# Seven-product value projections in the second half of block 1 as well, with sums of the context made in block 0

## The chip, the cores and the metric

The kernel runs on one core of one Trainium2 chip. The metric is the device time of one execution in microseconds, the median of three runs. Engines are named as in the profile: PE is TensorE (its weight loads are PEld), DVE is VectorE, ACT is ScalarE, POOL is GpSimd, and SP is SyncE, which issues nearly all transfers (its rows are marked SPq).

## The reference

```python
# x: 32 x 64 x 512, ctx: 32 x 64 x 512, H = 32 heads of DH = 128
q = (layernorm(x) @ Wq).reshape(b, lq, h, dh)
k = (ctx @ Wk).reshape(b, lk, h, dh)
v = (ctx @ Wv).reshape(b, lk, h, dh)
score = einsum('bqhd,bkhd->bhqk', q, k) * scale + position_bias   # masked keys: -inf
probs = softmax(score)                                            # masked keys: 0
x = x + tanh(g_xattn) * (einsum('bhqk,bkhd->bqhd', probs, v).reshape(b, lq, h * dh) @ Wo)
x = x + tanh(g_ffn) * (layernorm(x) @ weight.T + bias + lora(layernorm(x)))
```

The part that the change touches is `v`: the context (512 columns) times `Wv` (512 x 4096).

## The kernel before

**Precision.** Each float32 operand of a product is split into a high part (rounded by ACT, `hi`) and a rest (subtracted by DVE or POOL, `lo`, L1426 on POOL and L1151 on DVE). A product takes three matmuls: high times high, high times rest, rest times high (`mm3`, L395 to L398).

**Blocks and slots.** The 2048 rows are four blocks of 512 (8 batches). For each block the 32 heads are gone through, one head to a slot: 128 slots, slot n is head n % 32 of block n // 32. In a slot PE does the queries (12 matmuls of 128x512), the keys (12), then "main jobs" (24 matmuls: either two tiles of values for a group of four heads, or two tiles of the output projection), some small jobs in some slots (turning the normalised rows for the next block or the feed-forward part, the LoRA part, the dense part), then the scores of head n and last the attention of head n - 1. In block 0 the weights come raw from HBM, are split, used, and written back to HBM in split form (`wq_split` and so on); the later blocks load the split forms. So in slots 0 to 31 ACT and POOL also split each head's query and key weights, and in two slots of four POOL splits two chunks of the next group's value weights (`weights_v`).

**Programs by hand.** Each engine has its own instruction stream, written slot by slot, and waits on semaphores. In ACT's slot n come, in this order: the high part of the values of head n - 1 (`head_values`, v_hi), of the queries, of the next query weights, of the value or output weights, of the keys, of the next key weights, then the probabilities of head n - 1 (pt), a piece of the context or of the feed-forward weights, the first part of a round (below), copies of values out of PSUM, the turned rows, half the attention result (attn), the exponentials of head n, and the high part of the attention (ot_hi). In POOL's slot: the bias plus mask (L1466), the rest of the values (v_lo, L1485), the rests of the weights, of a piece, of a round, `deviations`, then the shift by the row maximum (L1515), the rest of the attention (ot_lo), the scaling of the probabilities (L1529), and last a round's four additions. DVE's slot has the rests of queries and keys, the transposes of the probabilities between them, their rest (pt, L1220), the statistics, the additions out of PSUM, and the scores.

**Seven products.** From pair 8 on (`FIRST_PAIR`; a pair is two groups of four heads, 8 slots, so pairs 8 to 15 are blocks 2 and 3) the values of a pair are not computed chunk by chunk. The 512x512 context and the 512x1024 weights are taken as 2x2 blocks, and seven block products replace eight (Strassen's scheme in Winograd's form): a pair takes 7 products x 2 tiles x 2 chunks x 3 = 84 matmuls in place of 2 groups x 4 tiles x 4 chunks x 3 = 96. The products of a pair lie in the slots 8u - 4 (four tiles), 8u - 1 and 8u (three each) and 8u + 3 (four); the first pair of all has the four tiles of 8u - 4 in 8u - 3 and 8u - 2 instead, two in each. Three of the products need only context and weights, four need mixed context (`sums`, from `ctxt_mixed`) and four need mixed weights (`wv_mixed`).

**Rounds.** The mixed operands are made in "rounds". A weights round takes 256 columns of two chunks for a pair into `raw_vo`, a context round takes two chunks that lie in `stage` anyway. POOL does four additions in place at the end of its slot n (`mix`, L1505). In slot n + 1 ACT rounds half 0 into `mixed_hi` after the probabilities and POOL subtracts it; SP writes both parts to HBM at the end of its slot n + 1. Half 1 uses the same `mixed_hi`, so ACT must wait until the write of half 0 has landed:

```python
def mixed_part(n, k):                                       # ACT, L1006
    act.wait_ge(mix_done, 4 * (r + 1))
    wait(act, mix_hi_saved, 16 * (2 * r + k))
```

For a round before `NEXT_SLOT` (50) half 1 follows at the end of ACT's and POOL's slot n + 1 (L1095, L1560), ahead of the high parts of slot n + 2; for later rounds it comes in the middle of slot n + 2 (L1072). SP writes half 1 in slot n + 2 (n + 3 for the late ones), waits there for all four writes (`mix_saved`), and then loads the next round's weights or the next two pieces of context. The rounds of before: weights in slots 33, 35 to 49, 55, 60, 64, 68, 72, 76, 80 (16), context in 52, 57, 84, 89 (4).

**SP's slot** around this: write back split value or output weights (`save_pair`), wait for the rests of the next query and key weights, write them back and load the next raw ones (`head`), write half 1 of a round, load the bias, load raw value or output weights (`raw_pair`, each load waits until POOL is done with that buffer), product loads, pieces, and last half 0 of a round (`save_mixed(n - 1, 0)`).

Of the kernel before, what the change touches and what calls it, by code (L numbers as in the profile page):

```python
# [15 lines left out]
P = 128  # L16
# [78 lines left out]
PIECES = 28  # L95

PAIRS = GROUPS // 2
FIRST_PAIR = 8
HALF = BLK // 2
PRODUCTS = (1, 2, 6, 7, 4, 3, 5)  # L100
CONTEXT_SIDE = {1: (0, 0), 2: (2, 0), 4: (2, 1)}
SUM_SIDE = {6: (0, 0), 7: (0, 1), 5: (1, 1), 3: (1, 0)}
WEIGHT_SIDE = {1: (0, 0), 2: (0, 2), 3: (1, 2)}
MIXED_SIDE = {6: (1, 1), 7: (0, 1), 4: (1, 0), 5: (0, 0)}
T_ROUNDS = [*range(33, 50, 2), 55, *range(60, 81, 4)]
S_ROUNDS = [H * b + s for b in (1, 2) for s in LEAD_PIECES[1::2]]
ROUNDS = sorted(T_ROUNDS + S_ROUNDS)
NEXT_SLOT = 50


def products_at(n):
# [26 lines left out]
def in_next(n):  # L138

    for m, late in ((n - 1, False), (n - 2, True)):  # L140
        if round_at(m) and late == (m >= NEXT_SLOT):
            return m
    return None


def round_at(n):
# [99 lines left out]
def flamingo_block(nc, x, ctxt, pair_bias, mask, wq, wk, wv, wo, g_xattn, g_ffn, wf, fbias, lora_a, lora_b,  # L246
                   lora_starts, lora_const, out):
    with ExitStack() as ctx:
# [30 lines left out]
                              for m in "vo")  # L279

        wv_mixed = nc.dram_tensor("wv_mixed", [FIRST_GROUPS // 2, 2, 2, 2, P, 2, G * DH], F32, kind="Internal").ap()
        ctxt_mixed = nc.dram_tensor("ctxt_mixed", [2, 2, 2, 2, P, BLK], F32, kind="Internal").ap()

        qt = two("qt", [P, BLK])
        kt = sb("kt", [P, PB, 2, P], F32R)
# [121 lines left out]
        def _(sp):  # L407
# [102 lines left out]
            def save_mixed(n, k):  # L510

                r, what, i = round_at(n)
                for part, src, split, saved in ((0, f32(mixed_hi[:, :]), mix_hi, mix_hi_saved),
                                                (1, mixed(what)[k][:, :], mix_lo, mix_lo_saved)):
                    sp.wait_ge(split, 2 * r + k + 1)
                    if what == "context":
                        sp.dma_start(ctxt_mixed[i // 2, k, i % 2, part], src).then_inc(saved, 16)
                    else:
                        sp.dma_start(wv_mixed[i // 4, k, :, i % 4 // 2, :, part, cols(i % 2, HALF)].rearrange("w p d -> p w d"),
                                     src.rearrange("p (w d) -> p w d", w=2)).then_inc(saved, 16)  # L520

            def load_weights(i):

                if i == 0:
                    sp.wait_ge(wo_lo, G * FIRST_GROUPS)
                else:
                    mix_saved(ROUNDS.index(T_ROUNDS[i - 1]))
                for k in range(2):
                    src = wv.rearrange("(g c) p d -> g c p d", c=C)[2 * (i // 4):2 * (i // 4) + 2, 2 * k + i % 4 // 2]
                    sp.dma_start(raw_vo[k][:, :].rearrange("p (g d) -> p g d", g=2),  # L530
                                 src[:, :, cols(i % 2, HALF)].rearrange("g p d -> p g d")).then_inc(weights_in[k], 16)

            def load_product(number):

                u, p = FIRST_PAIR + number // len(PRODUCTS), PRODUCTS[number % len(PRODUCTS)]
                if number < 2:
                    sp.wait_ge(vo_ps, NUMBER["v", 2 * FIRST_PAIR - 1, PB - 1] + 1)
                else:
                    v, q = FIRST_PAIR + (number - 2) // len(PRODUCTS), PRODUCTS[(number - 2) % len(PRODUCTS)]
                    sp.wait_ge(vo_ps, NUMBER["w", v, q, 1] + 1)  # L540
                if p in WEIGHT_SIDE:
                    l, c = WEIGHT_SIDE[p]
                    first = C * ((2 * u + l) % FIRST_GROUPS) + c
                    src = wv_split[first:first + 2].rearrange("c p d -> p c d")
                else:
                    mix_saved(ROUNDS.index(T_ROUNDS[4 * (u % 4) + 3]))
                    src = wv_mixed[u % 4, MIXED_SIDE[p][0], MIXED_SIDE[p][1]].rearrange("k p a d -> p k (a d)")
                sp.dma_start(f32(v_both[:, cols(number % 2, 2), :, :]).rearrange("p c a d -> p c (a d)"),
                             src).then_inc(product_in[number % 2], 16)

            def load_sums(u, p):
# [2 lines left out]
                    sp.wait_ge(wq_lo, H)  # L554
                    sp.wait_ge(wk_lo, H)
                if p in (6, 7):
                    mix_saved(ROUNDS.index(S_ROUNDS[2 * (u // 4) - 3]))
                    if u > FIRST_PAIR:
                        sp.wait_ge(vo_ps, NUMBER["w", u - 1, 5 if p == 6 else 3, 1] + 1)
                else:  # L560
                    sp.wait_ge(vo_ps, NUMBER["w", u, 6 if p == 5 else 7, 1] + 1)
                at, (k, half) = int(p in (7, 3)), SUM_SIDE[p]
                sp.dma_start(f32(sums[:, at, :, :, :]).rearrange("p k a s -> p (k a) s"),
                             ctxt_mixed[u // 4 - 2, k, :, :, :, cols(half, HALF)].rearrange("k a p s -> p (k a) s")
                             ).then_inc(sums_in[at], 16)

            def product_loads(n):
# [48 lines left out]
            for n in range(SLOTS):  # L616
# [24 lines left out]
                if n == LORA_LOAD:  # L641
                    piece(2)
                    piece(3)
                elif at and not (at[1] == "context" and b > 0):
                    piece(at[0] + 2)
                if dense_at(n - 1):
                    for t in dense_at(n - 1)[1]:
# [9 lines left out]
                for m in (n - 2, n - 3):  # L657
                    if round_at(m) and (m == n - 3) == (m >= NEXT_SLOT):
# [2 lines left out]
                            load_weights(i + 1)  # L661
                        elif what == "context":
                            mix_saved(r)
                            piece(8 * (i // 2 + 1) + 6 + 2 * (i % 2))
                            piece(8 * (i // 2 + 1) + 7 + 2 * (i % 2))
                if round_at(n - 1):
                    save_mixed(n - 1, 0)
            for t in range(PB):
# [965 lines left out]
```

## Time and profile before

| | us |
|---|---|
| median of three runs | 1724.39 (1724.36 to 1726.24) |
| the profiled execution | 1725.24 |
| its span in the profile | 1723.4 |
| PE busy, share of the span | 99% |
| DVE | 71% |
| POOL | 52% |
| ACT | 40% |
| mean granted TensorE clock | 0.999 of full speed |

The span is the time from the first to the last instruction of the profiled execution; 1.8 us lie around it. A matmul's row gives its duration from start to end, but matmuls are pipelined, so what one adds to PE's time is the distance of two starts. Slots are found in PE's timeline by the first `q_bank<-xt` matmul of each.

### The profile page before, as it was taken

What the parts mean: (1) busy time and instruction counts of PE and PEld (TensorE: products, weight loads), DVE (VectorE), ACT (ScalarE), POOL (GpSimd) and SP (SyncE); (2) the same over time, 40 slices, a digit from 0 to 9 for tenths busy, and PEclk for the clock granted to TensorE, in tenths of its full rate; (3) what the DMA queues carried; (4) which work ended last, traced back from release to release, by engine and by line L of the source; (5) the groups of instructions that cost most, each with busy time, mean ns of one, the idle gap of its engine ahead of it and who ended that gap; (6) DMA issues with size and microseconds to landing.
All of it is one profiled execution on the core that took longest, in us unless ns stands there. A gap on an engine that the chain in (4) does not pass through costs nothing.

```text
span 1723.4 us, 25737 instructions
## 1 busy us (share of the span) xinstructions
PE 1701.1 (99%) x8522; PEld 1436.2 (83%) x8522; DVE 1224.5 (71%) x2648; ACT 693.3 (40%) x1473; POOL 902.0 (52%) x1187
## 2 busy tenths in 40 slices
PE   8999999999999999999999999999999999999998
PEld 6788888888888888888888888888888888888886
DVE  5777767777676665666777777577777777777775
ACT  5545556554334442444333433233333333333331
POOL 5767767765566653654455653454534444343431
PEclk9999999999999999999999999999999999999999
DMA  7777778766677774756777776586766666666541
GB/s 278 270 258 271 260 267 288 270 244 226 211 241 240 251 235 158 257 210 236 250 248 286 274 277 237 169 319 244 267 224 242 220 228 247 224 218 242 198 142 44
DMA packets 162856, 407.95 MB, mean 237 GB/s; under 512 B 15554, under 2 KB 56642, under 8 KB 162724
## 3 DMA queue, kind: packets, MB, share of 16 engines
q1 hardware_dynamic: 162580, 406.05, 67.3%
q8 instruction: 69, 1.13, 0.3%
q14 instruction: 63, 0.52, 0.1%
q10 hardware_dynamic: 144, 0.26, 0.0%
HBM read 313.97 MB, written 92.27 MB: 236 GB/s over the span
## 4 chain that ended last, share of the span: by engine, by line
PE 89%; DVE 4%; issue 2%; POOL 2%; ACT 1%; DMA 1%; SPq 0%; DVEq 0%; ACTq 0%; POOLq 0%
PE vo_bank L396 12%; PE vo_bank L398 12%; PE vo_bank L397 12%; PE q_bank L396 7%; PE q_bank L398 7%; PE q_bank L397 7%; PE k_bank L397 6%; PE k_bank L398 6%; PE k_bank L396 6%; PE s_two L401 5%; PE pv_two L401 4%; PE s_two L402 2%; PE pv_two L402 2%; DVE score L1233 1%; DVE pv_two L1213 1%
## 5 line engine op out<-in xcount | busy, mean ns | idle before, releaser
L1515 POOL TENSOR_TENSOR score<-score,row_max 128x256 f32<-128x256 f32 x128 | 78.8, 616 | 553.8 <-DVE row_max L1238 553.8
L1426 POOL TENSOR_TENSOR ot_lo<-attn,ot_hi 128x512 fp32r<-128x512 f32 x128 | 165.8, 1296 | 174.9 <-ACT ot_hi L928 174.9
L1024 ACT ACTIVATE attn<-pv_two 128x512 f32<-128x512 f32 x128 | 76.6, 599 | 374.5 <-PE pv_two L402 374.4
L396 PE MATMUL q_bank<-xt_hi,wq 128*128 128x512 f32 x512 | 208.4, 407 | 0.0
L398 PE MATMUL q_bank<-xt_hi,wq 128*128 128x512 f32 x512 | 200.7, 392 | 0.0
L397 PE MATMUL q_bank<-xt_lo,wq 128*128 128x512 f32 x512 | 200.0, 391 | 0.0
L396 PE MATMUL k_bank<-ct_hi,wk 128*128 128x512 f32 x512 | 199.5, 390 | 0.3 <-DVE ct_lo L1151 0.3
L397 PE MATMUL k_bank<-ct_lo,wk 128*128 128x512 f32 x512 | 199.2, 389 | 0.0
L398 PE MATMUL k_bank<-ct_hi,wk 128*128 128x512 f32 x512 | 199.2, 389 | 0.0
L396 PE MATMUL vo_bank<-wo,ot_hi 128*128 128x512 f32 x496 | 193.1, 389 | 1.0 <-POOL ot_lo L1426 1.0
L398 PE MATMUL vo_bank<-wo,ot_lo 128*128 128x512 f32 x496 | 193.0, 389 | 0.0
L397 PE MATMUL vo_bank<-wo,ot_hi 128*128 128x512 f32 x496 | 193.0, 389 | 0.0
L1485 POOL TENSOR_TENSOR v_lo<-values,v_hi 128x256 fp32r<-128x256 f32 x256 | 189.5, 762 | 0.4 <-ACT v_hi L984 0.4
L1151 DVE TENSOR_TENSOR qt_lo<-q_bank,qt_hi 128x512 fp32r<-128x512 f32 x128 | 88.5, 692 | 141.9 <-ACT qt_hi L928 141.9
L1213 DVE STREAM_TRANSPOSE pv_two<-score 32x128 f32<-32x128 f32 x512 | 165.3, 323 | 9.6
L1233 DVE SCALAR_TENSOR_TENSOR score<-s_two,raw_bias 64x256 f32<-64x256 f32 x256 | 107.6, 420 | 77.3 <-PE s_two L402 74.7
L1018 ACT ACTIVATE pt<-pv_two 64x256 fp32r<-64x256 f32 x256 | 97.0, 379 | 124.4 <-DVE pv_two L1213 122.1
L401 PE MATMUL s_two<-kt,qt_hi 128*128 128x256 f32 x512 | 127.5, 327 | 7.1 <-issue 6.6
L928 ACT ACTIVATE kt<-k_bank 128x512 fp32r<-128x512 f32 x128 | 76.3, 596 | 135.0 <-PE k_bank L398 135.0
L401 PE MATMUL pv_two<-pt,v_hi 128*128 128x256 f32 x512 | 130.5, 332 | 0.0
L1220 DVE TENSOR_TENSOR pt<-pv_two,pt 64x256 fp32r<-64x256 f32 x256 | 108.1, 422 | 26.5 <-ACT pt L1018 24.8
L1175 DVE TENSOR_TENSOR acc<-vo_bank,acc 128x512 f32<-128x512 f32 x124 | 84.7, 691 | 56.3 <-PE vo_bank L398 54.3
(218 smaller groups left out, 4201.8 us busy)
## 6 DMA issues: line engine op xcount, KB each, us to landing
wq<-wq_split SPq DMA_DIRECT2D x96, 512.0 KB, 3.3
wk<-wk_split SPq DMA_DIRECT2D x96, 512.0 KB, 3.6
wo<-wo_split SPq DMA_DIRECT2D x96, 512.0 KB, 5.6
wv<-wv_mixed SPq DMA_DIRECT2D x32, 1024.0 KB, 7.8
wv<-wv_split SPq DMA_DIRECT2D x24, 1024.0 KB, 6.9
raw_bias<-in_pair_bias SPq DMA_DIRECT2D x64, 256.0 KB, 5.9
wq_split<-wq SPq DMA_DIRECT2D x32, 512.0 KB, 2.9
wk_split<-wk SPq DMA_DIRECT2D x32, 512.0 KB, 4.2
```

The costliest lines, as they stand in the source:

```text
L396: pe.matmul(to, left[0], right[0], start=first, stop=False)
L397: pe.matmul(to, left[0], right[1], start=False, stop=False)
L398: return pe.matmul(to, left[1], right[0], start=False, stop=last)
L401: pe.matmul(to, left[0], right, start=True, stop=False)
L1018: last = act.activation(pt[rows, :, 0, rows], turned[rows, :, :], ACT.Copy)
L1151: dve.tensor_tensor(to, src, f32(of), ALU.subtract).then_inc(done, 1)
L1175: dve.tensor_tensor(acc[b % 2][:, t, :], bank_of(job)[:, :], acc[b % 2][:, t, :], ALU.add).then_inc(vo_free, 1)
L1213: last = dve.transpose(turned[to, :, cols(i, S // 2)], score[of, :, cols(1 - i, S // 2)])
L1220: last = dve.tensor_tensor(pt[rows, :, 1, rows], turned[rows, :, :], f32(pt[rows, :, 0, rows]), ALU.subtract)
L1233: last = dve.scalar_tensor_tensor(out=score[rows, :, :], in0=s_two[rows, :, part, rows], scalar=SCALE, in1=plus[rows, :, :], op0=ALU.mult, ...
L1426: pool.tensor_tensor(to, src, f32(of), ALU.subtract).then_inc(done, 1)
L1485: last = pool.tensor_tensor(v[1][:, cols(half, 2), :], values_f[:, v_block(g, half), :, cols(h, DH)], f32(v[0][:, cols(half, 2), :]), ALU. ...
```

## The change

Pairs 6 and 7, the second half of block 1, get seven products too, so ten pairs have them. Context rounds are also made in block 0 (slots 20 and 25) from the pieces of block 1's context, and `ctxt_mixed` gets a third block. The 16 weights rounds lie in slots 33 to 51 at every second slot and 54 to 64 at every second slot. All rounds finish in slot n + 1 (`NEXT_SLOT = SLOTS`). The mixed weights are made in the order of the pairs 2, 3, 0, 1, as they are wanted. In block 0 the next pieces are loaded after a round's writes, as in the other blocks.

```diff
-FIRST_PAIR = 8
+FIRST_PAIR = 6
-T_ROUNDS = [*range(33, 50, 2), 55, *range(60, 81, 4)]
-S_ROUNDS = [H * b + s for b in (1, 2) for s in LEAD_PIECES[1::2]]
+T_ROUNDS = [*range(33, 52, 2), *range(54, 65, 2)]
+S_ROUNDS = [H * b + s for b in range(BLOCKS - 1) for s in LEAD_PIECES[1::2]]
-NEXT_SLOT = 50
+NEXT_SLOT = SLOTS
+def pair_of_round(i):
+
+    return (FIRST_PAIR + i // 4) % (FIRST_GROUPS // 2)
-        ctxt_mixed = nc.dram_tensor("ctxt_mixed", [2, 2, 2, 2, P, BLK], F32, kind="Internal").ap()
+        ctxt_mixed = nc.dram_tensor("ctxt_mixed", [BLOCKS - 1, 2, 2, 2, P, BLK], F32, kind="Internal").ap()
-                        sp.dma_start(wv_mixed[i // 4, k, :, i % 4 // 2, :, part, cols(i % 2, HALF)].rearrange("w p d -> p w d"),
+                        sp.dma_start(wv_mixed[pair_of_round(i), k, :, i % 4 // 2, :, part, cols(i % 2, HALF)].rearrange("w p d -> p w d"),
-                    mix_saved(ROUNDS.index(T_ROUNDS[4 * (u % 4) + 3]))
+                    mix_saved(ROUNDS.index(T_ROUNDS[4 * min(u - FIRST_PAIR, 3) + 3]))
-                    mix_saved(ROUNDS.index(S_ROUNDS[2 * (u // 4) - 3]))
+                    mix_saved(ROUNDS.index(S_ROUNDS[2 * (u // 4) - 1]))
-                             ctxt_mixed[u // 4 - 2, k, :, :, :, cols(half, HALF)].rearrange("k a p s -> p (k a) s")
+                             ctxt_mixed[u // 4 - 1, k, :, :, :, cols(half, HALF)].rearrange("k a p s -> p (k a) s")
-                elif at and not (at[1] == "context" and b > 0):
+                elif at and at[1] != "context":
                     piece(at[0] + 2)
-                            piece(8 * (i // 2 + 1) + 6 + 2 * (i % 2))
-                            piece(8 * (i // 2 + 1) + 7 + 2 * (i % 2))
+                            piece(8 * (i // 2) + 6 + 2 * (i % 2))
+                            piece(8 * (i // 2) + 7 + 2 * (i % 2))
```

## Rows read from the trace of the kernel before

**Rows 1.** The page's part 1: busy time of each engine.
```profile
PE 1701.1 (99%) x8522; PEld 1436.2 (83%) x8522; DVE 1224.5 (71%) x2648; ACT 693.3 (40%) x1473; POOL 902.0 (52%) x1187
```

**Rows 2.** The waits of PE: waiter, releaser, total us, times, longest us.
```profile
PE s_two L401 <- issue: 6.6, 5, 3.7
PE vo_bank L817 <- DVE acc L1175: 4.2, 5, 1.5
```

**Rows 3.** Timeline of PE in slot 55: start us, us, instruction.
```profile
739.86 0.39 PE L396 MATMUL k_bank<-ct_hi,wk 128*128 128x512 f32 x1
...
746.43 0.39 PE L398 MATMUL vo_bank<-wv,ct_lo 128*128 128x512 f32 x1
...
747.53 0.33 PE L401 MATMUL pv_two<-pt,v_hi 128*128 128x256 f32 x1
```

**Rows 4.** Windows of slots 56, 57, 63, 68, 89, 95, 2 and 3.
```profile
core 0: us, PE busy (x) PEld busy (x) DVE busy (x) ACT busy (x) POOL busy (x), PEclk, DMA share, GB/s
...
748.45:761.21 12.76, 12.76 (x66) 10.86 (x66) 7.38 (x18) 6.35 (x13) 9.74 (x13) 1.00 0.71 246
761.21:776.09 14.88, 13.39 (x70) 11.17 (x70) 11.62 (x25) 5.74 (x12) 8.83 (x12) 1.00 0.46 161
...
846.77:858.20 11.43, 11.43 (x60) 9.67 (x60) 9.03 (x21) 4.00 (x9) 4.77 (x7) 1.00 0.77 262
907.97:921.04 13.07, 13.01 (x67) 10.77 (x66) 10.55 (x23) 5.08 (x11) 5.16 (x8) 1.00 1.00 390
1186.90:1200.92 14.02, 13.37 (x70) 11.17 (x70) 10.92 (x25) 5.33 (x11) 7.12 (x10) 1.00 0.63 240
1266.67:1278.34 11.67, 11.65 (x60) 9.65 (x60) 9.26 (x22) 3.99 (x9) 4.77 (x7) 1.00 0.55 196
37.34:49.43 12.09, 8.36 (x43) 7.03 (x42) 7.88 (x20) 7.25 (x15) 10.51 (x12) 0.94 0.87 316
49.43:63.09 13.66, 13.66 (x67) 11.51 (x66) 8.41 (x18) 7.38 (x15) 8.88 (x11) 0.93 0.89 317
```

**Rows 5.** Timeline of POOL in slot 56, which starts at 748.45.
```profile
753.88 3.20 POOL L1505 TENSOR_TENSOR raw_vo<-raw_vo 128x256 f32<-128x256 f32 x4
757.04 0.74 POOL L1466 TENSOR_TENSOR raw_bias<-raw_bias,mask_add 128x256 f32<-128x256 f32 x1
757.74 1.43 POOL L1485 TENSOR_TENSOR v_lo<-values,v_hi 128x256 fp32r<-128x256 f32 x2
...
760.37 1.28 POOL L1426 TENSOR_TENSOR raw_vo<-raw_vo,mixed_hi 128x512 f32<-128x512 f32 x1
```

**Rows 6.** Timeline of POOL at slot 22, which starts at 292.77.
```profile
290.04 2.54 POOL L1426 TENSOR_TENSOR wv<-raw_vo,wv 128x512 fp32r<-128x512 f32 x2
294.43 0.62 POOL L1515 TENSOR_TENSOR score<-score,row_max 128x256 f32<-128x256 f32 x1 [1.85 <-DVE row_max L1238]
```

**Rows 7.** Timeline of SP at the end of its slot 21.
```profile
291.36 1.87 SPq L409 DMA_DIRECT2D raw_vo<-in_wv  x2
```

**Rows 8.** DMA issues: KB each, median us from issue to landing.
```profile
ctxt_mixed<-mixed_hi SPq DMA_DIRECT2D x8, 256.0 KB, 4.7
```

**Rows 9.** The line L517, which issues the context rounds' writes.
```profile
DMA to landing us min/median/max: 3.2/4.6/7.5
```

**Rows 10.** Timeline of ACT in slot 22.
```profile
295.92 0.71 ACT L984 ACTIVATE v_hi<-values 128x256 fp32r<-128x256 f32 x2
...
300.19 0.77 ACT L1018 ACTIVATE pt<-pv_two 64x256 fp32r<-64x256 f32 x2
```

**Rows 11.** Timeline of DVE in slot 22.
```profile
301.00 0.86 DVE L1220 TENSOR_TENSOR pt<-pv_two,pt 64x256 fp32r<-64x256 f32 x2 [0.17 <-ACT pt L1018]
```

**Rows 12.** Timeline of POOL at slot 27, which starts at 359.53.
```profile
361.44 0.61 POOL L1515 TENSOR_TENSOR score<-score,row_max 128x256 f32<-128x256 f32 x1 [2.66 <-DVE row_max L1238]
```

**Rows 13.** Timeline of SP at the end of its slot 26.
```profile
358.38 0.99 SPq L409 DMA_DIRECT2D raw_vo<-in_wo  x2
```

**Rows 14.** Timeline of ACT in slot 27.
```profile
362.93 0.71 ACT L984 ACTIVATE v_hi<-values 128x256 fp32r<-128x256 f32 x2
```

**Rows 15.** Timeline of DVE in slot 27.
```profile
368.65 0.86 DVE L1220 TENSOR_TENSOR pt<-pv_two,pt 64x256 fp32r<-64x256 f32 x2 [0.17 <-ACT pt L1018]
```

More of the change, by code:

```diff
@@ L528, in load_weights @@
                 for k in range(2):
-                    src = wv.rearrange("(g c) p d -> g c p d", c=C)[2 * (i // 4):2 * (i // 4) + 2, 2 * k + i % 4 // 2]
+                    src = wv.rearrange("(g c) p d -> g c p d", c=C)[2 * pair_of_round(i):2 * pair_of_round(i) + 2, 2 * k + i % 4 // 2]
                     sp.dma_start(raw_vo[k][:, :].rearrange("p (g d) -> p g d", g=2),
```

## The prediction

> **What bounds the kernel now.** I read the page's busy times first: PE is busy for 1701.1 of 1723.4 us [rows 1]. Then PE's waits: the longest line is 6.6 us in all, the next 4.2 us [rows 2]. So PE is the bound almost everywhere, and what counts is how many matmuls it runs and whether each finds its operands. PE's timeline gives the price of a matmul: 29 distances of starts from 739.86 to 746.43 us, 0.2266 us each [rows 3]. The windows by slot give the cost of each kind of slot: a plain slot 12.76 us, a slot with three product tiles 11.43, with four 13.07, and 11.67 for a three-tile slot behind a slot that turns rows [rows 4]. POOL, SP, ACT and DVE matter only where they come later than PE wants them, so their timelines are read against PE's place in the slot: the attention of a slot starts 0.93 us before its end (747.53, with slot 56 starting at 748.45) [rows 3, 4].
>
> **Block 1, what goes away.** Each new pair saves 12 matmuls, 24 x 0.2266 = 5.4 us. By slots: 47, 48, 55 and 56 become three-tile slots, 4 x (11.43 - 12.76) = -5.3 us. The twelve plus twelve matmuls of the first pair's first product tiles move from slots 61 and 62 to 45 and 46, which have turning jobs as well; that comes to nothing. Slots 52, 59 and 60 get four tiles in place of a plain job and cost 13.07 - 12.76 = 0.31 each, 0.9 us together; the scores follow there after only two tiles and wait for DVE's rest of the keys. Slot 47 now follows a turning slot: +0.24.
>
> **Block 1, what the rounds cost.** The number of weights rounds stays 16, so POOL, ACT and SP do the same work, at other times. The four additions take 3.16 us of POOL (753.88 to 757.04), and v_lo, which PE's attention wants, then ends at 757.74 + 1.43 = 759.17, 10.72 us into the slot [rows 5]. In a plain slot PE wants it at 12.76 - 0.93 = 11.83, so it hides. In a three-tile slot PE wants it at 11.43 - 0.93 = 10.50. The rounds 47, 54 and 62 now lie just ahead of three-tile slots (48, 55, 63): 0.22 us and a semaphore's delay, say 0.28 each, +0.8 us. Slots 52, 57 and 58 get a round right behind another, so the second half's subtraction (1.28) comes ahead of the four additions and v_lo ends near 12.0, against 11.83 in slot 53 and about 12.1 or later in 58 and 59: some 0.2. ACT's rounding of the second half (0.6) now comes ahead of the high parts in slots 47, 51, 56, 59, 60 and 64; before the early rounds were hidden in plain slots, in product slots it may show as 0.05 to 0.1. I take 0.5 for all of this, with bounds 0 and 2.5 (six such slots at 0.3, plus slots 53, 58, 59 at 0.2). Slot 57 took 14.88, its like in the next block 14.02 [rows 4]; the difference is an ACT rounding of the late kind in its middle, which goes away, and the slot ahead is of the three-tile kind as there: -0.9. Block 1 in sum: -5.3 + 0.2 + 0.9 + 0.8 + 0.5 - 0.9 = **-3.8 us**.
>
> **Block 0, the two added rounds.** They are four additions each (3.16 us of POOL), two roundings on ACT, two subtractions on POOL (1.28 each), and four writes on SP, and they fall where POOL also splits query, key and value weights. The work itself is not the issue; the order is.
> Round 20: POOL's additions run at the start of slot 21's work, so the value weights' rests end at 292.58 + 3.16 = 295.7, the first half's subtraction at 297.0, and the shift, at 294.43 before, comes 2.6 us late [rows 6]. SP's second load of raw value weights waits for the same rests: its issues ended at 293.23 [rows 7], now near 296.4. Only behind it does SP issue the write of `mixed_hi`. Such a write lands 4.7 us later [rows 8], near 301.1. ACT waits for exactly this landing before it may round the second half (0.6), and behind that stand, in order, v_hi, the queries, the weights, the keys, and pt. So v_hi, at 295.92 before, starts near 301.7, 5.8 us late, and what follows it has no idle time of this size before pt at 300.19 [rows 10]. The rest of pt ended at 301.86 on DVE [rows 11], now near 307.7, and PE wants it at 305.53 - 0.93 = 304.6. PE loses 3.1 us in slot 22. DVE then still has statistics, two additions and the scores to do, so the shift of slot 23 is late by some 2.5 us, of which I let 0.4 reach PE there.
> Round 25: SP's raw load ended at 359.37 [rows 13]; POOL's value weights' rests, which it waits for, come 3.16 later, so the write goes out near 362.4 and lands near 367.1. With the rounding v_hi starts near 367.7, 4.8 late against 362.93 [rows 14]; the rest of pt, ended at 369.51 [rows 15], is ready at 374.3, and PE wants it at 372.27 - 0.93 = 371.3: 3.0 us.
> Block 0 in sum: 3.1 + 0.4 + 3.0 = **+6.5 us**. Bounds: if ACT never waited for the landing, POOL's lateness alone is left. It is 2.6 us in slot 22, and 3.16 + 1.28 - 2.66 = 1.8 in slot 27 [rows 12]; DVE and ACT have about 1 us of slack behind it, so 0 to 2.5 us. At the slowest write of the kernel (7.5) [rows 9] each round costs 2.8 more, 12 in all; at the quickest (3.2) 1.5 less each, 3.5. I take the median, since the writes go out right behind other loads, as most do.
> SP also waits in slots 22 and 27 until a round's writes have landed, with the next pieces behind that wait and then the write-back of value weights. The pieces are wanted two slots later, the write-backs three; nothing. The 2 MB of extra writes are 0.5% of the traffic; nothing.
> A rule of the Trainium skill speaks for a smaller price. DMA: Bandwidth & Descriptors, section Anatomy of one DMA, fits a transfer (for the path through GpSimd) as about 2.0 us plus bytes over 436 GB/s. For 256 KB that is an estimate of 2.6 us in place of the row's 4.7; the two rounds would then cost some 4 us less and the time would come out near 1723. The trace disagrees: no such write of this kernel lands in under 3.2 us.
>
> **Sum.** -3.8 + 6.5 = +2.7 us on the profiled execution's 1725.24, 1727.9 (span 1726.1). That execution lies 0.85 above the median of 1724.39, so the median is forecast at **1727.1**: block 1 gives back what the title promises, and block 0 takes more. 0.2% (3.45 us) is about what a measurement of this kernel can tell from no change: 1720.9 and 1727.8 are its ends, and the forecast lies near the upper one.
>
> **Rivals.**
> *The cover of block 0 holds* (the other side). If the write's issue is not held up by SP's raw load, or lands by 295.9, ACT rounds in time and PE loses 0 to 2.5 us: 1720.6 to 1723.1. For it: ACT idles in long stretches, and the early rounds of block 1 run without any pause of PE. Against: in block 1 POOL has no weights to split. It decides where the landing comes before 5.8 us into slot 22: above this every us of landing is one of PE's.
> *TensorE's clock falls too.* In slot 2 PE pauses for 3.7 us [rows 2], and the granted clock is 0.94 there and 0.93 in slot 3, which takes 13.66 instead of 12.76 [rows 4]: 0.9 us. The new pauses are of nearly that length. If both do the same: +1.8, 1728.9. Against: they split into a wait at the scores and a short one at the attention. The Trainium skill, TensorE: Matmul & The Clock Gate, section Why this matters for your kernels, says that pauses between bursts of matmuls bring the engine back to its lower clock (1.2 of 2.4 GHz); the trace agrees for slot 2 and is silent on shorter pauses.
> *The rounds jam.* In slots 51 to 60 five rounds follow each other, and each waits for the write of the one before. If SP, which waits for landings there, falls behind by half a slot, the four additions wait for their weights and v_lo is late by 2 us in two or three slots: +4, 1731.
>
> **How the numbers follow.** Forecast 0.40 (its own range 1724.5 to 1729), cover holds 0.26, clock 0.14, jam 0.12, something else 0.08. Faster by over 0.2% needs the cover to hold fully: 0.13. Slower takes the upper part of the forecast's range (0.15), nearly all of clock and jam, some of the rest: 0.42. Same: 0.45. The range from 1720.5 to 1731.5 leaves out about a tenth on each side.
>
> **What would show it.** PE's count falls by 24. In the new profile slots 22 and 27 are about 16 us long, with PE's scores waiting, ACT's v_hi starting 8 to 9 us into the slot behind a rounding into `mixed_hi`. Slots 47, 48, 55 and 56 are 11.4 to 11.8 us. I am wrong if slots 22 and 27 stay under 14 us, or if product slots of block 1 exceed 12.3.

## The result, and the profile after

The changed kernel took **1767.27 us** (median, 1764.56 to 1770.98) against 1725.07 (1724.36 to 1726.24) of the kernel before, measured beside it: a ratio of 1.0244, 95% interval 1.0232 to 1.0257. It is 42 us slower. The forecast was 1727.1, the range ended at 1731.5. PE runs the 24 matmuls fewer that the change promises, and yet it is busy for longer than before [rows 1]: part of them ran slower, as is shown below. Line numbers of the changed kernel are up to 5 higher than those of before.

The page of the changed kernel, part 1 (busy time) and part 4 (the chain that ended last, by engine):

```profile
PE 1716.6 (97%) x8498; PEld 1444.3 (82%) x8498; DVE 1243.5 (70%) x2676; ACT 687.6 (39%) x1465; POOL 910.5 (51%) x1199
...
PE 78%; DVE 6%; issue 5%; POOL 4%; DMA 4%; ACT 2%; SPq 1%; DVEq 0%; ACTq 0%; POOLq 0%
```

The waits of the changed kernel (waiter, releaser, total us, times, longest us):

```profile
ACT mixed_hi L933 <- issue: 21.8, 6, 5.8
PE s_two L406 <- issue: 20.5, 13, 5.4
...
ACT mixed_hi L933 <- DMA wv_mixed<-mixed_hi: 12.0, 5, 5.2
...
PE vo_bank L822 <- DVE acc L1180: 9.8, 6, 5.4
```

PE's waits of before, 6.6 and 4.2 us [rows 2], have become 20.5 and 9.8, and behind them stands ACT, which waits 34 us (21.8 and 12.0) before it writes the one buffer `mixed_hi`. (Where the profile names no releaser, "issue", the wait ends within 0.1 us of the landing of the last write out of that buffer, in all six cases.) To place the loss I took the start of each slot (its first query matmul) from PE's timelines of both kernels and subtracted the lengths. The slots of the profiled execution sum to +44.2 us: **14.6 us in block 0** (slot 22 +5.5, 23 +1.1, 27 +7.2, 28 +1.4) and **29.9 us in block 1** (45 to 51 +13.3, 52 and 53 +6.1, 54 to 64 +10.5). All other slots together differ by 0.3 us. Five of them, as windows of the changed kernel (slots 22, 27, 45, 52 and 60):

```profile
core 0: us, PE busy (x) PEld busy (x) DVE busy (x) ACT busy (x) POOL busy (x), PEclk, DMA share, GB/s
294.13:312.39 18.26, 14.57 (x66) 12.35 (x66) 9.19 (x22) 6.58 (x14) 15.28 (x16) 0.88 0.71 245
366.96:386.88 19.92, 14.55 (x67) 12.36 (x66) 10.12 (x23) 7.67 (x16) 13.12 (x14) 0.90 0.72 255
607.74:631.39 23.65, 18.24 (x83) 15.07 (x82) 9.90 (x22) 6.30 (x13) 6.46 (x9) 0.86 0.72 253
726.72:745.54 18.82, 14.64 (x66) 11.71 (x66) 10.80 (x23) 6.33 (x13) 10.41 (x14) 0.91 0.95 365
...
843.58:863.72 20.14, 15.77 (x66) 12.89 (x66) 10.78 (x23) 5.70 (x12) 6.42 (x9) 0.83 0.88 313
```

Slots 22, 27, 52 and 60 were 12.74 to 12.76 us, slot 45 13.21. Besides a PE without work, the column PEclk is to be seen: 0.83 to 0.91, where slots of these kinds had 1.00 before [rows 4].

**Slot 45.** The timeline of SP's queue in the changed kernel (start us, us, instruction; in brackets, where there is one, the idle time before it and what ended it):

```profile
606.14 0.88 SPq L553 DMA_DIRECT2D wv<-wv_split  x2
607.07 0.47 SPq L414 DMA_DIRECT2D stage<-in_ctxt  x1
607.58 0.62 SPq L524 DMA_DIRECT2D wv_mixed<-mixed_hi  x1
```

The timeline of ACT:

```profile
616.77 0.63 ACT L933 ACTIVATE mixed_hi<-raw_vo 128x512 fp32r<-128x512 f32 x1 [5.79 <-issue]
617.31 0.71 ACT L989 ACTIVATE v_hi<-values 128x256 fp32r<-128x256 f32 x2
617.92 0.58 ACT L933 ACTIVATE qt_hi<-q_bank 128x512 fp32r<-128x512 f32 x1
618.40 0.59 ACT L933 ACTIVATE kt<-k_bank 128x512 fp32r<-128x512 f32 x1
```

The timeline of PE:

```profile
624.28 1.09 PE L822 MATMUL vo_bank<-ident,xn 128*128 128x128 f32 x4 [5.41 <-DVE acc L1180]
625.02 0.78 PE L401 MATMUL q_bank<-wv,ct_hi 128*128 128x512 f32 x1
...
626.02 0.63 PE L403 MATMUL q_bank<-wv,ct_lo 128*128 128x512 f32 x1
626.45 0.63 PE L401 MATMUL q_bank<-wv,ct_hi 128*128 128x512 f32 x1
...
628.89 0.40 PE L401 MATMUL vo_bank<-wv,ct_hi 128*128 128x512 f32 x1
```

In slot 44 the first pair of the new set loads its two first operands. SP waits for the last value tile before it issues them (606.14), and each is 1 MB. Only behind these and a load of 256 KB does SP issue the write of round 43's rounded half (607.58). The trace has this write land after 9.1 us (the same line had at most 7.6 us before), at 616.7, behind the two loads, which took 5.9 and 8.8 us, and at 616.77 ACT may round the second half into the one buffer. v_hi, qt_hi and kt stand behind it in order, DVE behind these, and PE stands for 5.41 us. Then PE runs at the lower of its two clock levels: starts 0.43 us apart (626.02 to 626.45) where 0.2266 is the price at the higher [rows 3]. Nine distances of starts take 3.87 us there (625.02 to 628.89), where 9 x 0.2266 = 2.04 is their price at the higher level: another 1.8 us. So slot 45 loses 10.4 us, of which 12 x 0.2266 = 2.7 are matmuls that moved here, 5.4 the wait, and some 2 the clock. The Trainium skill, TensorE: Matmul & The Clock Gate, section "Wait — 56ns, not 53.3ns?", gives 426.7 ns from start to start at 512 columns on the cold array; the trace agrees with its 0.43.

Slots 47, 54, 56, 60 and 64 show the same ACT wait (2.13, 5.14, 1.90, 5.24, 2.19 us). **Slot 52 is different.** The timeline of SP's queue:

```profile
722.51 3.90 SPq L553 DMA_DIRECT2D wv<-wv_split  x2
726.46 1.16 SPq L600 DMA_DIRECT2D out<-acc  x2
727.71 0.90 SPq L535 DMA_DIRECT2D raw_vo<-in_wv  x2
```

The timeline of POOL, and then that of ACT:

```profile
737.37 3.13 POOL L1510 TENSOR_TENSOR raw_vo<-raw_vo 128x256 f32<-128x256 f32 x4 [4.87 <-DMA raw_vo<-in_wv]
```
```profile
740.53 0.63 ACT L933 ACTIVATE mixed_hi<-raw_vo 128x512 fp32r<-128x512 f32 x1 [4.66 <-POOL raw_vo L1510]
741.18 0.60 ACT L1005 ACTIVATE values<-vo_bank 128x512 f32<-128x512 f32 x1
```

Here round 51's raw weights are issued at 727.71, behind two product loads whose issue took 3.9 us with its wait; they land 8.8 and 9.1 us later (median 5.3 before), POOL makes its additions at 737.37, ACT waits for them, and behind ACT's rounding stands the copy that would empty PE's product bank (a wait of 4.1 us on PE).

### The profile page after: what moved, and what is told of

Same layout as the page of the kernel before. It is cut to its first block, busy times and chain, and to the rows that moved or that the text cites. A ratio compares the mean times of both kernels' runs of the same rounds, so it can differ in the third digit from the quotient of the medians.

```text
span 1769.2 us, 25764 instructions
## 1 busy us (share of the span) xinstructions
PE 1716.6 (97%) x8498; PEld 1444.3 (82%) x8498; DVE 1243.5 (70%) x2676; ACT 687.6 (39%) x1465; POOL 910.5 (51%) x1199
## 4 chain that ended last, share of the span: by engine, by line
PE 78%; DVE 6%; issue 5%; POOL 4%; DMA 4%; ACT 2%; SPq 1%; DVEq 0%; ACTq 0%; POOLq 0%
PE vo_bank L401 10%; PE vo_bank L402 10%; PE vo_bank L403 10%; PE q_bank L401 7%; PE q_bank L402 6%; PE q_bank L403 6%; PE k_bank L401 5%; PE k_bank L402 5%; PE k_bank L403 5%; PE s_two L406 4%; PE pv_two L406 4%; DMA wv_mixed<-mixed_hi 2%; DVE score L1238 2%; PE s_two L407 1%; PE pv_two L407 1%
## 5 line engine op out<-in xcount | busy, mean ns | idle before, releaser
L406 PE MATMUL s_two<-kt,qt_hi 128*128 128x256 f32 x512 | 131.7, 335 | 21.2 <-issue 20.5
L406 PEld LDWEIGHTS s_two<-kt,qt_hi 128*128 128x128 f32 x512 | 98.6, 193 | 35.9 <-issue 32.0
```

The source lines that it names most:

```text
L406: pe.matmul(to, left[0], right, start=True, stop=False)
```

## The experiments

All times are medians in us; beside each set of runs the kernel before was measured again (1723.7 to 1725.2), and the ratios are to that. "Block 0" and "block 1" are the sums of slot differences, 17 to 31 and 45 to 64, of each profiled execution. The kernel changed as given has +14.6 and +29.9. Without the waits block 1 would be near the forecast's -3.8.

**1. Two buffers.** Each half of a round rounds into a buffer of its own, so ACT waits for a write of the round before, not of the same one. Room comes from placing two small tiles of the LoRA step in existing buffers.

```
-                wait(act, mix_hi_saved, 16 * (2 * r + k))
+                wait(act, mix_hi_saved[k], 16 * r)
...
-                hi(mixed_hi[:, :], mixed(what)[k][:, :], mix_hi)
+                hi(mixed_hi[k][:, :], mixed(what)[k][:, :], mix_hi)
```

> The changed kernel with two buffers for the rounded half of a round, each with its own semaphore, so ACT no longer waits for the landing of half 0's write before it rounds half 1; two small LoRA scratch tiles move into buffers that are idle at that time, to make room. Theory W (ACT's wait for that landing, with everything behind it on ACT, is the loss): slots 22, 27, 45, 47, 54, 60 and 64, which lost 5.5, 7.2, 7.7, 2.3, 3.9, 7.1 and 2.0 us, come within 1.5 us of their price without the wait; slot 52, where POOL waited for a raw weight load, stays; the time falls from 1767 to 1725 to 1733. Rival P (POOL's additions and subtractions themselves come too late): those slots stay long and the time stays over 1755. Rival D (the product slots are too dense for DVE and the banks): slots 45 and 47 stay long, the others go.

**2. Block 0's rounds alone.** FIRST_PAIR, T_ROUNDS and NEXT_SLOT as before the change:

```
-FIRST_PAIR = 6
+FIRST_PAIR = 8
...
-T_ROUNDS = [*range(33, 52, 2), *range(54, 65, 2)]
+T_ROUNDS = [*range(33, 50, 2), 55, *range(60, 81, 4)]
...
-NEXT_SLOT = SLOTS
+NEXT_SLOT = 50
```

> The kernel before with the two context rounds of block 0 alone (slots 20 and 25, their sums never read), products and other rounds as before. Theory W: slots 22, 23, 27 and 28 grow by the same 5.5, 1.1, 7.2 and 1.4 us as in the changed kernel and nothing else moves: 1739 to 1740. Rival D (products are to blame) has no say here. Rival P expects the same sum. If the two rounds cost under 5 us alone, the loss in block 0 depends on something else of the change and both are wrong.

**3. The weight rounds' new places alone**, on the kernel before: eight sets as before, no rounds in block 0.

```
-T_ROUNDS = [*range(33, 50, 2), 55, *range(60, 81, 4)]
+T_ROUNDS = [*range(33, 52, 2), *range(54, 65, 2)]
...
-NEXT_SLOT = 50
+NEXT_SLOT = SLOTS
```

> The kernel before with the weights rounds of the changed kernel (33 to 51, 54 to 64, every second slot) and all second halves finished in the next slot, eight pairs of products as before, no rounds in block 0. Theory W: slots 54 and 60, where SP has waits or large loads ahead of the write, lose again (4 and 7 us or similar in a neighbour), slots 45 and 47 do not, since no product loads stand in slot 44 and 46: 1732 to 1745. Rival D (products of pairs 6 and 7): nothing lost, 1724 to 1726. Rival P: as W in sum, but POOL and not ACT is waited for.

**4. The write earlier.** One buffer; SP issues the write of the first half's rounded part ahead of the slot's head loads (block 0) or product loads.

```
+                if n >= H and round_at(n - 1):
+                    save_mixed(n - 1, 0, (0,))
                 product_loads(n)
```

> The changed kernel with one buffer, but SP issues the write of half 0's rounded part earlier: before the waits for the next head's weights in block 0, and before the product loads in the other blocks. Theory W: the landing comes 3 us or more earlier in slots 22, 27 and 45, and earlier in 47, 54 and 60, so these slots lose under 2 us each where they lost 5 to 8; the time falls to 1728 to 1745. Rival P and rival D: no change, 1760 to 1770.

Measured:

```
                     us                        ratio [interval]        block 0  block 1
1 two buffers        1740.33 (1738.36-1742.46) 1.0092 [1.0077, 1.0107]   +10.6    +3.9
2 block 0's rounds   1737.45 (1736.28-1738.39) 1.0075 [1.006, 1.009]     +12.0    -0.1
3 rounds moved       1732.66 (1731.89-1733.42) 1.0048 [1.0033, 1.0063]    +1.7    +5.6
4 write earlier      1741.08 (1738.19-1744.82) 1.01   [1.0081, 1.012]     +9.8    +4.7
```

Another buffer and another place in SP's queue have in common that ACT no longer waits for the landing, and both take 26 to 27 us away; block 1's sum falls by 25 to 26. The fourth also shows what made the landing late. These are the times to landing of slot 44's write, first in the changed kernel and then in the fourth experiment, where it goes out ahead of the two 1 MB loads:

```profile
DMA to landing us min/median/max: 9.1/9.1/9.1
```
```profile
DMA to landing us min/median/max: 4.2/4.2/4.2
```

In the same way the two moved writes of block 0 land after 2.5 and 2.0 us in place of 5.7 and 6.1, and those of slots 46, 50, 52, 53 and 57 after 2.2 to 2.5 in place of 5.1 to 8.9.

Not all came as expected. The first ends 7 us above its theory's range, since slots 23, 24 and 28 now lose 4.5, 1.0 and 3.0 us. In the second, slots 27 and 28 grow as in the changed kernel, but 22 and 23 by 1.9 and 2.3 us in place of 5.5 and 1.1, and the time stays under the 1739 to 1740 that were expected. The third lies inside its theory's range, but slots 54 and 60, named for the loss, lose nothing; 57, 58, 59 and 64 take 1.3, 0.8, 0.5 and 2.3 us.

The waits of the kernel with two buffers no longer hold ACT's for its own write; two others are left:

```profile
ACT mixed_hi L937 <- POOL raw_vo L1515: 15.1, 14, 4.6
...
PE s_two L409 <- issue: 12.1, 9, 3.5
...
POOL raw_vo L1515 <- DMA raw_vo<-in_wv: 8.7, 5, 4.8
...
PE vo_bank L404 <- ACT values L1009: 4.0, 1, 4.0
```

Experiments 2 and 3 give 12.0 and 5.6 us, so some 24 us of block 1's 29.9 come only with the new sets and their loads on top of the rounds' places; the places alone are no disaster. (The new sets without the moved rounds were not run.) (The 1.7 us of block 0 in experiment 3 are in slot 25, which its edit does not touch: such a difference comes and goes.)

What block 0 loses once the landing is out of the way was not in my sum. From the end of slot 21 into slot 23 of the kernel with two buffers (slot 23 starts at 308.59), the timelines of POOL, ACT and PE, one after the other:

```profile
288.16 3.21 POOL L1515 TENSOR_TENSOR stage<-stage 128x256 f32<-128x256 f32 x4
...
309.29 2.55 POOL L1436 TENSOR_TENSOR wv<-raw_vo,wv 128x512 fp32r<-128x512 f32 x2
```
```profile
318.72 1.29 ACT L937 ACTIVATE wo<-raw_vo 128x512 fp32r<-128x512 f32 x2 [2.62 <-issue]
```
```profile
323.28 0.36 PE L409 MATMUL s_two<-kt,qt_hi 128*128 128x256 f32 x1 [3.53 <-issue]
```

POOL has nearly no gap from 288 to 312; its rests of the value weights end at 311.8, SP may load the next raw output weights only then, ACT's splitting of them waits 2.62 us with the keys behind it, and PE's scores wait 3.53. So a second cause: POOL's time and order in slots that split value weights. And a third is slot 52, still +6.2.

**5 to 7. Lighter slots for block 0; no round at 51; both.** On the kernel with two buffers.

```
+def lead_pieces(b):
+    return LEAD_PIECES if b > 0 else (22, 23, 26, 27)
```
```
-T_ROUNDS = [*range(33, 52, 2), *range(54, 65, 2)]
+T_ROUNDS = [*range(33, 50, 2), *range(54, 67, 2)]
```

> The kernel with two mixed_hi buffers, with block 0's context pieces at slots 22, 23, 26, 27 in place of 19, 20, 24, 25: the mixing then lies in slots 23 and 27, and POOL's rests in slots 24 and 28, where it splits no value weights. Theory (POOL's three extra operations push its value-weight rests late, which delays SP's next raw loads and with them ACT's output-weight halves and DVE): of block 0's 11 us over the kernel before at most 3 stay, 1731 to 1734 us. Rival (any slot of block 0 is full, the work costs what it costs wherever it stands): 8 or more stay, 1737 to 1741 us.

> Two mixed_hi buffers; the weight round of slot 51 is left out and all later ones are two slots later (last one at 66), so that no weight round stands right ahead of the context round of slot 52. Theory (slot 52's 6.2 us are the raw weight load that SP issues behind a product load's wait, with ACT's rounding standing in order before its copies of product tiles): slot 52 is back within 1 us of the kernel before, 1733 to 1735 us. Rival (slot 52 is long because the moved product tiles and the context pieces fill it): it keeps over 4 us, or they turn up in a neighbour slot, 1738 to 1741 us.

> Both edits together with two mixed_hi buffers. Theory: the losses are apart and add, so that block 0 costs up to 3 us and slot 52 none, against some 4 to 5 us gained by the 24 products: 1721 to 1728 us. Rival (a loss that is taken from one place shows up in the next): 1732 us or more.

```
                     us                        ratio [interval]        block 0  slots 52, 53
5 block 0 lighter    1736.93 (1734.43-1741.45) 1.0065 [1.0048, 1.0082]    +7.4    +7.2
6 no round at 51     1733.75 (1733.03-1735.07) 1.0052 [1.0037, 1.0067]    +9.7    +0.3
7 both               1731.8  (1730.22-1733.49) 1.004  [1.0025, 1.0055]    +5.3    +0.3
```

The sixth bears slot 52 out: 0.3 us. The fifth misses its theory's range (1731 to 1734) and ends at the edge of its rival's (1737 to 1741): the loss left slots 22, 23, 27 and 28 but 4.6 to 6.0 us of it turned up in slot 25, where PE waits for normalised rows. In the trace of the seventh POOL, still working off the round of slot 23, comes to its part of them at 345.8 us, 15 us into the slot. So the seventh misses its theory's range too (1721 to 1728) and ends at the edge of its rival's (1732 or more): a loss that is taken from one place shows up in another. In the seventh, moreover, slots 48 and 49 take 1.9 and 2.3 us more. SP issues round 47's raw weights at 642.73, after the landing of the round before; they reach POOL in slot 48 (641.65 to 656.35), with v_lo behind the additions. The timelines of POOL and of PE there:

```profile
649.30 3.18 POOL L1519 TENSOR_TENSOR raw_vo<-raw_vo 128x256 f32<-128x256 f32 x4 [2.29 <-DMA raw_vo<-in_wv]
...
653.12 1.41 POOL L1499 TENSOR_TENSOR v_lo<-values,v_hi 128x256 fp32r<-128x256 f32 x2
```
```profile
654.59 0.58 PE L413 MATMUL pv_two<-pt,v_hi 128*128 128x256 f32 x1 [2.23 <-POOL v_lo L1499]
...
656.35 0.73 PE L408 MATMUL q_bank<-xt_hi,wq 128*128 128x512 f32 x1
...
657.31 0.63 PE L410 MATMUL q_bank<-xt_hi,wq 128*128 128x512 f32 x1
657.74 0.63 PE L408 MATMUL q_bank<-xt_hi,wq 128*128 128x512 f32 x1
...
661.15 0.42 PE L410 MATMUL q_bank<-xt_hi,wq 128*128 128x512 f32 x1
```

Again a wait, of 2.2 us, and then matmuls 0.43 us apart: eleven distances take 4.80 us in slot 49 (656.35 to 661.15), 2.3 more than 11 x 0.2266, which is all that slot 49 loses. Here the slow stretch costs at least as much as the wait.

**8 and 9. Block 0 at slots 19 and 27; rounds 47 and 49 at 48 and 50.**

```
-    return LEAD_PIECES if b > 0 else (22, 23, 26, 27)
+    return LEAD_PIECES if b > 0 else (18, 19, 26, 27)
```
```
-T_ROUNDS = [*range(33, 50, 2), *range(54, 67, 2)]
+T_ROUNDS = [*range(33, 46, 2), 48, 50, *range(54, 67, 2)]
```

> As the kernel of both edits (two mixed_hi buffers, no weight round at 51), but block 0's context pieces at slots 18, 19, 26, 27: the first round mixes in slot 19 instead of 23, its rests lie in slot 20, and slot 25, which waited 4.5 us for the normalised rows because POOL came to its deviations at 345.8 us, has no mixing before it. Theory (block 0's loss is POOL's order and load in a few slots): block 0 stands within 2 us of the kernel before, 1726 to 1729 us. Rival (the same microseconds turn up around slot 20 to 22, where POOL is as full): block 0 keeps 4 us or more, 1730 us and over.

> As that, and the weight rounds of slots 47 and 49 a slot later, at 48 and 50. Theory (in the kernel of both edits the round of slot 47 had its raw weights only at 649.3 us, in slot 48, its four additions stood ahead of v_lo, TensorE waited 2.2 us and then ran 11 matmuls at the lower clock: 4.2 us in slots 48 and 49): an extra slot for that load takes 3 to 4 us away, 1722 to 1726 us. Rival (the round's late raw load follows from DMA traffic of slot 47 to 50, wherever the round is): slots 48 to 51 keep 3 us or more, 1727 us and over.

The eighth took 1728.38 (1726.07 to 1731.61), ratio 1.0021 [1.0012, 1.003]: block 0 +5.4, block 1 -2.1. Its time fits its theory and its block 0 the rival. The ninth took 1725.7 (1723.97 to 1727.55), 1.0002 [0.9992, 1.0011]: block 0 +2.7, block 1 -3.1, slots 48 and 49 as forecast. Their block 0 is the same code, so its loss varies by up to 2.7 us from one execution to another; on it the eighth decides nothing.

**10. The new places with one buffer**, to see whether good places alone would do.

> The changed kernel with its one mixed_hi buffer, with the rounds where the last one has them (block 0 at slots 19 and 27, weight rounds 33 to 45, 48, 50, 54 to 66). Theory (the wait of ACT for the landing of mixed_hi is a cost of its own, in every round whose first write SP issues behind waiting or large loads): the losses of slots 45, 47, 54, 56, 60 and 64 come back, some 20 to 27 us above the kernel with two buffers, 1742 to 1753 us. Rival (the wait only hurt together with the crowded rounds, and the new places hide it): 1726 to 1732 us.

1768.27 (1767.82 to 1768.78), 1.0252 [1.0239, 1.0265], blocks +15.8 and +24.8: worse than either expected. The buffer is worth 43 us with these places. Slot 52, with no round at 51, is 6.1 us longer again, and slot 21 8.5. There, the timelines of ACT and of PE:

```profile
292.58 0.63 ACT L937 ACTIVATE mixed_hi<-stage 128x512 fp32r<-128x512 f32 x1 [8.70 <-issue]
```
```profile
297.71 0.55 PE L410 MATMUL s_two<-kt,qt_hi 128*128 128x256 f32 x1 [6.60 <-issue]
```

**11. Two buffers and the write early**, at the new places.

> The kernel with two buffers and the new places, and SP writes half 0's rounded part before the slot's product and stage loads too. Theory (with two buffers no wait for a landing is left that reaches TensorE): no change within 1 us, 1724 to 1727 us. Rival (the writes' landing still sets when the next raw weights come): 1721 to 1723 us, faster than the kernel before.

1725.26 (1722.78 to 1731.2), 1.0002 [0.9993, 1.001]: no change against the ninth. No landing of the first write reaches PE any more.

**12. Block 0's additions shortened**, at the change's own places, with two buffers. Block 1's context sums are left out (8 of 256 columns are added); all waits, roundings, rests and writes stand.

```
+                    if n < H:
+                        to, left, right = to[:, 0:8], left[:, 0:8], right[:, 0:8]
                     pool.tensor_tensor(to, left, right, op).then_inc(mix_done, 1)
```

> The kernel with two mixed_hi buffers and the change's own places; in block 0's two rounds the four additions work on 8 columns instead of 256, so that block 1's context sums are not computed, while ACT's roundings, POOL's two rests, SP's writes and all waits stand as they were. Theory (block 0's 11 us are POOL's time, 3.2 us of it these additions in each round): block 0 keeps 3 to 6 us of the 11, 1732 to 1736 us. Rival (they are ACT's roundings or SP's and the queues' extra writes): block 0 keeps 9 us or more, 1738 to 1741 us.

1734.74 (1732.9 to 1738.48), 1.0064 [1.0049, 1.0078]. Block 0 falls from +10.6 to +3.2, within the theory's range. The medians say the same: 16.6 us over the kernel before in experiment 1, 9.6 here. A round's four additions still take 1.05 us in place of 3.19, so 4.3 us less of POOL in two rounds give about 7 us of the end time: in these slots POOL's lateness costs more than its own length.

**13 to 15. The additions on DVE instead.** DVE makes the context rounds' four additions at the end of the slot: in block 0 alone (13, otherwise as the ninth), in all blocks (14), in block 0 at the change's own slots 20 and 25 (15).

```
                 row_scales(n)
+                if round_at(n) and mix_on_dve(n):
+                    mix(dve, n)
```

> Two mixed_hi buffers, the new places (block 0 at slots 19 and 27, weight rounds 33 to 45, 48, 50, 54 to 66), and DVE instead of POOL makes the four additions of block 0's two context rounds, at the end of the slot after row_inv, where it has 1 us or more without work. Theory (the 3 to 4 us that block 0 still costs are POOL's time): block 0 keeps 0 to 1.5 us, 1722.5 to 1724.5 us. Rival (they are the roundings, rests and queues, or DVE gets as late as POOL was): 1725 us or more.

> As that, in all three blocks: the additions of the context rounds of slots 52, 57, 84, 89 are DVE's too. Theory: POOL was no bound in those slots, DVE has room, within 1 us of the kernel with block 0's sums alone on DVE. Rival (slots 52 and 57, where PE waits for DVE's acc 1.0 us, get longer): 1 us or more above it.

> Two buffers, DVE's additions in block 0, but the rounds of block 0 at the change's own slots 20 and 25 (weight rounds at the new places). Theory (POOL's time in slots 20 to 28, where it splits value weights): nothing left out, as with additions of 8 columns block 0 costs 3 to 5 us, 1725 to 1728 us. Rival (DVE's own 1.5 us make its output halves and keys late in the same slots): block 0 keeps 7 us or more, 1730 us or more.

```
                       us                        ratio [interval]        block 0  block 1
13 block 0 on DVE      1722.29 (1720.24-1724.42) 0.9979 [0.997, 0.9988]     0.0    -3.1
14 all on DVE          1727.0  (1724.4-1730.29)  1.0011 [1.0002, 1.0019]    0.0    -1.4
15 own places, DVE     1727.13 (1725.4-1730.82)  1.0014 [1.0005, 1.0023]   +5.7    -3.4
```

**The thirteenth beats both kernels**: 2.6 us under the one before (0.2%), 45 under the one changed as given. Block 0 has the lengths of before, and block 1 gains 3.1. Block 0 alone would not prove it, since it varies by 2.7 us; the medians of 10 and 11 executions do, 0.7 us over the kernel before in the ninth and 2.6 under it here. Its additions (timeline of DVE, slot 19) take about as long as POOL's 3.2 us, but they stand where little waits:

```profile
270.58 0.18 DVE L1282 RECIPROCAL row_inv<-row_sum 128x4 f32<-128x4 f32 x1
270.68 3.06 DVE L435 TENSOR_TENSOR stage<-stage 128x256 f32<-128x256 f32 x4
```

One addition alone can be much quicker on DVE. The line of the additions, engine by engine (ns, least, median and most), and POOL's timeline at the same time:

```profile
L435 POOL TENSOR_TENSOR stage<-stage x16: 730/737/741, 718.2 to 1206.1; 128x256 f32<-128x256 f32 x16
L435 DVE TENSOR_TENSOR stage<-stage x8: 395/572/1410, 270.7 to 378.0; 128x256 f32<-128x256 f32 x8
```
```profile
270.69 1.54 POOL L1463 TENSOR_TENSOR ot_lo<-attn,ot_hi 128x512 fp32r<-128x512 f32 x1 [1.05 <-ACT ot_hi L962]
```

In all ten rounds that DVE adds in experiments 13 to 15, the first addition took 0.40 us and the second, begun while POOL's ot_lo ran, 1.40 to 1.50. So it seems that the 3.06 us are long because POOL works beside DVE; no run with POOL at rest there was made, so this is not shown.

The fourteenth goes to its rival, by 4.7 us: slots 58 and 90, right behind a round with DVE's additions, turn rows, and PE then waits for DVE. The timeline of PE in slot 58:

```profile
790.17 0.63 PE L851 MATMUL vo_bank<-ident,xn 128*128 128x128 f32 x4 [1.94 <-DVE acc L1209]
```

The fifteenth fits its theory's time and misses its block 0 by a little: 5.7 us, 2.5 more than with shortened additions, where POOL's full ones cost 7.4 more.

## Why the prediction was wrong

**What held.** PE's count falls by 24. Where nothing stands in the way, block 1 gives about what the sum said: -3.1 to -3.8 us in experiments 9, 11, 13 and 15, against -3.8, though with rounds at other places than the sum was made for. By slots of experiment 13: 48 and 56 are 11.4, 55 11.7; 58 to 60 take 0.3 to 0.6 more each, 52 0.45. In block 0 the chain that was described is in the trace, step for step. In the changed kernel's slot 22 (294.13 to 312.39), the timelines of SP's queue, ACT and PE:

```profile
296.45 1.57 SPq L414 DMA_DIRECT2D raw_vo<-in_wv  x2
298.07 0.48 SPq L522 DMA_DIRECT2D ctxt_mixed<-mixed_hi  x1
```
```profile
303.81 0.63 ACT L933 ACTIVATE mixed_hi<-stage 128x512 fp32r<-128x512 f32 x1 [3.35 <-issue]
304.35 0.71 ACT L989 ACTIVATE v_hi<-values 128x256 fp32r<-128x256 f32 x2
```
```profile
308.94 0.55 PE L406 MATMUL s_two<-kt,qt_hi 128*128 128x256 f32 x1 [3.69 <-issue]
```

v_hi comes 10.2 us into the slot (forecast 8.9), the write lands after 5.7 us instead of the median 4.7 [rows 8], and PE waits 3.69 us (forecast 3.1). But this chain is not what block 0 costs: with the wait for the landing gone, experiments 1 and 4 still lose 10.6 and 9.8 of the 14.6 us there.

**The steps that failed.**
- *"ACT's rounding of the second half (0.6) ... in product slots it may show as 0.05 to 0.1. I take 0.5"*, the price of the moved rounds in block 1, with bounds 0 and 2.5. This is the main error. For block 0 I followed the one buffer to its landing; for block 1 I priced only the instruction, and I took the absence of a pause in the early rounds as evidence. Those lie in slots where SP issues the write with no product load ahead: ACT's two roundings stand 7.3 us apart there, more than a landing of 4.8. The new sets bring 1 MB loads into slots 44 to 63, ahead of the writes, with waits of their own. Experiments 1 and 4 show the step's true size: 25 to 26 us of block 1's 29.9.
- *"The trace disagrees: no such write of this kernel lands in under 3.2 us"* is too wide. It holds for the writes of the context rounds [rows 9]; those of the weights rounds, of the same 256 KB, landed from 2.2 us in the same trace, and experiment 4 has landings of 2.0 to 2.5 where no large load stood ahead. So the price depends on what SP has issued before the write, which the median hid.
- *"The rounds jam"*, the rival nearest to what happened: SP's queue falls behind, the additions wait for their weights. It has its place (slot 52, POOL 4.87 us for `raw_vo`) and experiment 6 bears it out, but it was priced at +4 in all; slot 52 alone cost 6.1, since ACT's copies of product tiles stand behind the rounding.
- *"TensorE's clock falls too"*, put at 0.9 us a pause and as a rival to the forecast. It was no rival: every PE wait of over 2 us read here was followed by a stretch at the lower level, which cost 1.8 us behind slot 45's wait and 2.3 in slot 49 of experiment 7. In block 0 (14.6 against 6.5) PE's waits of 3.7 and 5.4 us account for 3.0 of the miss (forecast 3.1 and 3.0); slots 22 and 27 lose 1.8 each beyond their waits, at a clock of 0.88 and 0.90, and slots 23 and 28 another 2.5.
- *"The cover of block 0 holds"*: with the landing gone, POOL's lateness alone was to cost 0 to 2.5 us. 10.6 us stay (experiment 1), about 7 of them for the additions (experiment 12). I followed it through one slot; it goes on, POOL to SP's next raw loads to ACT's splitting a slot later.

The sum also took each part by itself. Experiments 2 and 3, the rounds of block 0 and the moved rounds, lengthen the slots by 11.9 and 7.3 us; with the new products and their loads as the third part it is 44.2. Whether the remaining 25 us belong to that part alone or to its meeting with the others is not shown, since it was not run by itself.

Open stays what sets the up to 2.7 us by which block 0 differs between runs of the same code, and why the one buffer costs 43 us at the new places and only 27 at the change's own; I did not split that.

## What to carry to other kernels

A buffer that is written out and refilled by an engine in program order makes that engine wait for a DMA's landing; before moving it, read what its queue issues just ahead of the write in the new place, since large loads there can double the landing (9.1 us against a median of 4.8 here). Price a pause of the bound engine at its length plus the slow stretch behind it. Where an engine has no gaps over two slots, follow its lateness through the next slot's loads as well; the same work on another engine, in a slot where nothing waits for it, can be free though it takes as long.

## What the runs showed of the hardware

- A write of 256 KB, 4.8 us in the median, took 9.1 us when issued 1.4 us behind two loads of 1 MB on the same queue, and 4.2 us in experiment 4, ahead of them. Seven such writes with no large load just ahead took 2.0 to 2.5 us. The Trainium skill, DMA: Bandwidth & Descriptors, section Two DMAs through the same engine are not ordered, says that within one queue of one DMA engine descriptors start in order; the trace agrees in so far as the write did not pass the loads: they had landed after 5.9 and 8.8 us, by 615.4, the write at 616.7.
- After waits of 5.41 and 2.23 us TensorE started matmuls of 512 columns 0.43 us apart, nearly twice 0.2266, for some 4 us, which cost about 2: the lower of its two levels (1.2 of 2.4 GHz).
- Four dependent additions of 128x256 in fp32 took 3.06 us on DVE and mostly 3.1 to 3.2 on POOL. One alone took 0.73 to 0.75 us on POOL; on DVE 0.40 when it began with POOL's ot_lo, and 1.41 when it began while that ran, which then took 1.54 us.
